# Attention with unnormalised probabilities: values multiplied in PSUM by inverse denominators spread through memory

## What is computed

```python
q = _rope(_rmsnorm(q, q_norm_w), pos); k = _rope(_rmsnorm(k, k_norm_w), pos)
k_all = jnp.concatenate([kc, k], axis=1); v_all = jnp.concatenate([vc, v], axis=1)
scores = jnp.einsum('bqhd,bkhd->bhqk', q, k_all) * SCALE
scores = jnp.where(valid[:, None, None, :], scores, -1e+30)
probs = jax.nn.softmax(scores, axis=-1)
o = jnp.einsum('bhqk,bkhd->bqhd', probs, v_all)
return jnp.einsum('bse,de->bsd', o.reshape(bsz, seqlen, HQ * D), Wo)
```

## Time and profile before

| | before |
|---|---|
| median of 3 runs | 1417.21 us |
| the profiled execution's own time | 1418.94 us |
| its span | 1417.3 us |
| mean granted clock of TensorE | 0.991 |
| TensorE busy | 1363.1 us |
| DVE busy | 1104.8 us |
| ACT busy | 838.1 us |
| GpSimd busy | 456.1 us |

### The profile page before, as it was taken

How to read it: one execution, slowest core, us unless ns; L and a number is a source line. 1 busy time by engine, 2 the same in 40 slices (tenths; PEclk the granted TensorE clock), 3 DMA queues, 4 the chain that set the end, 5 groups by cost and what they waited for, 6 DMA issues and landing times.

```text
span 1417.3 us, 27566 instructions
## 1 busy us (share of the span) xinstructions
PE 1363.1 (96%) x7308; PEld 1157.6 (82%) x7308; DVE 1104.8 (78%) x2921; ACT 838.1 (59%) x1952; POOL 456.1 (32%) x485
## 2 busy tenths in 40 slices
PE   5999999989999999999999999999999999999995
PEld 4888888878888887888888877888888888888884
DVE  4532445869888889888888898888888988888883
ACT  5631334346666667756666677666657676666663
POOL 4000000355222336523333275222224552223320
PEclk9999999999999999999999999999999999999998
DMA  8111213372222235322222443222224522222210
GB/s 307 58 60 46 74 38 124 119 261 54 63 63 63 61 76 159 93 60 59 59 65 69 120 136 68 60 75 62 62 60 132 135 60 59 67 59 59 59 25 14
DMA packets 139828, 118.55 MB, mean 84 GB/s; under 512 B 90240, under 2 KB 109056, under 8 KB 139520
## 3 DMA queue, kind: packets, MB, share of 16 engines
q1 hardware_dynamic: 127328, 83.35, 21.1%
q0 software_dynamic: 11728, 34.09, 9.8%
q10 hardware_dynamic: 720, 0.54, 0.1%
HBM read 101.11 MB, written 16.78 MB: 83 GB/s over the span
## 4 chain that ended last, share of the span: by engine, by line
PE 85%; DVE 6%; issue 6%; ACT 1%; DMA 1%; POOL 0%; SPq 0%; DVEq 0%; POOLq 0%; ACTq 0%
PE bank L1399 16%; PE tail L1438 15%; PE wide L1468 12%; PE tail L1518 12%; PE wide L1433 8%; PE wide L422 4%; PE bank L1420 3%; PE wide L490 3%; PE tail L422 2%; PE bank L422 2%; PE wide L549 2%; DVE pr L1780 1%; PE bank L549 1%; PE bank L490 1%; PE tail L1491 1%
## 5 line engine op out<-in xcount | busy, mean ns | idle before, releaser
L1594 ACT ACTIVATE pr<-pr,nm,q_scale 128x640 f32<-128x640 f32 x256 | 235.6, 921 | 114.7 <-DVE nm L1763 113.8
L1438 PE MATMUL tail<-prT,vt 128*128 128x512 f32 x960 | 254.0, 404 | 4.2 <-DVE prT L1738 4.1
L1759 DVE CUSTOM_DVE_ANT_0 pr<-wide,bias 128x640 f32<-128x640 f32 x256 | 209.8, 819 | 13.6 <-issue 13.6
L1199 POOL TENSOR_TENSOR tick<-tick 128x1 f32<-128x1 f32 x127 | 30.1, 237 | 584.7 <-PE wide L1468 325.1
L1438 PEld LDWEIGHTS tail<-prT,vt 128*128 128x128 f32 x960 | 170.4, 188 | 44.5 <-DVE prT L1738 13.8
L1518 PE MATMUL tail<-woT,oT 128*128 128x512 f32 x768 | 197.2, 400 | 0.0
L1738 DVE TENSOR_TENSOR prT<-wide,prT 128x1024 fp32r<-128x1024 f32 x128 | 153.5, 1220 | 28.6 <-ACT prT L1586 27.8
L1468 PE MATMUL wide<-kT,qT 128*128 128x320 f32 x512 | 163.7, 320 | 4.4 <-DVE mx L1759 4.2
L1518 PEld LDWEIGHTS tail<-woT,oT 128*128 128x128 f32 x768 | 140.5, 189 | 27.1
L1468 PE MATMUL wide<-kT_low,qT 128*128 128x320 f32 x512 | 158.8, 310 | 0.0
L1468 PE MATMUL wide<-kT,oT 128*128 128x320 f32 x512 | 158.6, 310 | 0.0
(11 more groups left out here) (237 smaller groups left out, 2656.9 us busy)
## 6 DMA issues: line engine op xcount, KB each, us to landing
w_ring<-pair_weights SPq DMA_DIRECT2D x80, 256.0 KB, 3.8
k_raw<-k_pages SPq DMA_DIRECT2D x512, 32.0 KB, 2.1
v_raw<-v_pages SPq DMA_DIRECT2D x512, 32.0 KB, 1.7
xTb<-x_transposed POOLq DMA_DIRECT2D x31, 512.0 KB, 4.5
out<-y POOLq DMA_DIRECT2D x32, 256.0 KB, 4.0
rope<-rope_tables SPq DMA_DIRECT2D x31, 256.0 KB, 2.6
w_raw<-w_gate_up SPq DMA_DIRECT2D x10, 512.0 KB, 3.3
x_transposed<-xh SPq DMA_DIRECT2D x8, 512.0 KB, 4.6
```

The lines of the kernel that those rows point to most:

```text
L1438: last = nc.tensor.matmul(tail[g][:, :], vt[v_part][:, j, g * D:(g + 1) * D], prT[p_part][:, j, :], start=(j == 0 and v_part + p_part == 0 ...
L1594: ac.activation(pr[h][:, :], pr[h][:, :], ACT.Exp, bias=nm[:, h:h + 1], scale=q_scale[:, 0, head(h)], accum_out=den[:, h:h + 1]).then_inc( ...
L1759: v.tensor_tensor_reduce(halves(pr[h][:, :]), scores, halves(bias[:, :]), 1.0, -3.0e38, ALU.add, ALU.max, mx[:, h:h + 1]).then_inc(s_sfree, 1)
```

## The change

The probabilities stay as the exponential leaves them. The eight reciprocals are one operation on `den`, at the start of the next turn's back half on DVE. ACT stores them to a scratch tensor in memory (128 rows of eight values) and, after four of the squares, loads the whole of it back into every partition (`spread`, 4 KB each, over the place of the first two probability tiles). When the values of a key head are summed, DVE multiplies them in PSUM by `spread`, whose operand steps over the eight heads, and ACT and DVE then take high and low parts as before, ACT waiting for the multiplication. The low part of the second values stands after the first product of the second rotation. GpSimd waits for fewer things. The casts of weights on ACT are regrouped. In the "next" turn TensorE's ahead projections follow the common table. The pair loop is written out, three times, for PE, DVE and ACT. The semaphores of the probabilities go; three are new.

```diff
+    share_scratch = nc.dram_tensor("one_over_denominators", [P * HP], F32).ap()
...
+    spread = place(135168, "spread", [P, P, HP])
...
-    NSTEP = 22
+    NSTEP = 16
...
-    EARLY = {"next": ((0,), (1, 2, 3), (4, 5, 6, 7), (8,), (9,), (10,)), "out": ((), (), (), (12, 13), (14,), (15,)), None: ((),) * 6}
+    EARLY = {"next": ((0,), (1,), (2, 3), (4, 5, 6, 7), (8,), (9,), (10,)), "out": ((), (), (), (), (12, 13), (14,), (15,)), None: ((),) * 7}
...
-        with eng.Fori(0, NPAIR - 1) as pair:
+        for pair in range(NPAIR - 1):
             with eng.Fori(0, B - 2) as last:
...
             pool.wait_ge(s_sfull, u * HP + HP)
-            pool.wait_ge(s_p[0], u * SOON + FIRST)
...
                 pool.wait_ge(s_step, u * NSTEP + MASKED)
-                low_weights(own, first + 2, first + 3)
+                low_weights(own, first + 2, first + 4)
...
             if extra:
-                for h in range(REP):
-                    pool.wait_ge(s_p[0], u * SOON + h + 1 + FIRST)
-                    low_weights(own, first + 3 + h, first + 4 + h)
-                low_weights(own, first + 3 + REP, first + 2 * KT)
-
-        TURNED, MASKED = 2, NSTEP - SOON
+                low_weights(own, first + 4, first + 2 * KT)
+
+        TURNED, MASKED = 2, NSTEP
...
             def probs_wide(g, w):
 
-                pe.wait_ge(s_p[0], u * SOON + (SOON if g else REP) + FIRST)
-                if g:
-                    pe.wait_ge(s_p[1], u * LATE + LATE + FIRST)
+                pe.wait_ge(s_exp, u * HP + (HP if g else REP))
...
-                        ahead_to = AHEAD_NEXT if extra == "next" else AHEAD
-                        project_ahead(ahead_to[h], ahead_to[h + 1])
+                        project_ahead(AHEAD[h], AHEAD[h + 1])
...
             def copy_values(g):
-                act.wait_ge(s_pv, u * G + g + 1 + FIRST)
+                act.wait_ge(s_norm, u * G + g + 1)
                 ac.copy(oT[:, 0, g, :], tail[g][:, :]).then_inc(s_ohi, 1)
...
             if back:
                 high_probs(0, 0)
+                act.wait_ge(s_rden, u + 1)
+                act.dma_start(share_scratch.rearrange("(p h) -> p h", h=HP), rden[:, :]).then_inc(s_den, 16)
                 high_probs(0, 1)
 
                 act.wait_ge(j_full, u + 1)
                 ac.copy(prT[0][:, JT - 1, :], tail[1][:, :]).then_inc(s_phi, 1)
-                for h in range(SOON, HP):
-                    normalise(u, h)
             if front:
 
                 act.wait_ge(s_q0, n + 1)
                 squares(1, 0, REP)
+            if back:
+                act.wait_ge(s_den, u * 16 + 16)
+                act.dma_start(spread[:, :, :].rearrange("p q h -> p (q h)"),
+                              share_scratch.rearrange("(o n) -> o n", o=1).to_broadcast([P, P * HP])).then_inc(s_spread, 16)
...
             if back:
+                early(0)
                 high_probs(1, 0)
-                early(0)
+                early(1)
                 high_probs(1, 1)
...
+            def shares():
+
+                dve.wait_ge(s_exp, u * HP + HP)
+                v.reciprocal(rden[:, :], den[:, :]).then_inc(s_rden, 1)
+
+            def normalise(g):
+
+                dve.wait_ge(s_pv, u * G + g + 1 + FIRST)
+                if g == 0:
+                    dve.wait_ge(s_spread, u * 16 + 16)
+                summed = tail[g][:, :].rearrange("p (i q) -> p i q", i=REP)
+                v.tensor_tensor(summed, summed, spread[:, :, g * REP:(g + 1) * REP].rearrange("p q i -> p i q"), ALU.mult).then_inc(s_norm, 1)
...
             if back:
+                shares()
                 low_probs(0, 0)
...
                 low_probs(1, 1)
+                normalise(0)
                 low_new(1)
                 low_values(0)
...
             if back:
 
-                low_values(1)
+                normalise(1)
+                if not front:
+                    low_values(1)
             if front:
 
-                rotate(REP + G, REP, ((REP + G, REP, 0),)).then_inc(s_rope, 1)
+                rotate(REP + G, REP, ((REP + G, REP, 0),), (lambda: low_values(1)) if back else None).then_inc(s_rope, 1)
...
-                dve.wait_ge(s_p[1], n * LATE + FIRST)
                 for h in range(HP):
-                    mask_max(h, lambda: reciprocal(h - 2) if h >= 2 else None)
-                    if 2 <= h < REP + 2:
-                        normalise(h - 2)
-                for h in range(REP, SOON):
-                    normalise(h)
-                reciprocal(HP - 2)
-                reciprocal(HP - 1)
+                    mask_max(h)
```

More of the change, by code:

```diff
@@ L273, in build_program @@
                                     tick, xT, xh, x_tok, rope_all, token_place, s_x1, s_xl, s_ropemade, s_ropest, s_xs, s_init, m_full, m_free, s_grp,
-                                    x_scratch, rope_scratch, out)
+                                    x_scratch, rope_scratch, share_scratch, out)
         with nc.Block() as block:
@@ L1024, in build_attention @@
                     tick, xT, xh, x_tok, rope_all, token_place, s_x1, s_xl, s_ropemade, s_ropest, s_xs, s_init, m_full, m_free, s_grp,
-                    x_scratch, rope_scratch, out):
+                    x_scratch, rope_scratch, share_scratch, out):
     def place(offset, name, shape, dt=F32):
@@ L1082, in build_attention @@
     s_rden = sem("denominator_ready")
-    s_p = [sem(f"probs_ready{i}") for i in range(G)]
+    s_den = sem("one_over_denominators_stored")
+    s_spread = sem("one_over_denominators_spread")
+    s_norm = sem("values_normalised")
     s_pv = sem("values_summed")
@@ L1595, in exponential @@
                               accum_out=den[:, h:h + 1]).then_inc(s_exp, 1)
[L1597 to L1602, removed]
             def new_keys_values(n):
@@ L1629, in turn @@
                 squares(1, 0, REP)
+            if back:
+                act.wait_ge(s_den, u * 16 + 16)
+                act.dma_start(spread[:, :, :].rearrange("p q h -> p (q h)"),
+                              share_scratch.rearrange("(o n) -> o n", o=1).to_broadcast([P, P * HP])).then_inc(s_spread, 16)
+            if front:
                 arrive()
@@ L1651, in turn @@
                 copy_values(0)
-            early(1)
+            early(2)
             own = BACK[0] if back else 0
@@ L1655, in turn @@
                 copy_values(1)
-            early(2)
+            early(3)
             if front:
                 high(1, 2, qT[:, 0, :], bank[1][:, :])
-                early(3)
+                early(4)
                 high(0, 3 + own, kT[:, :, L:NK], bank[0][:, 0:G * S].rearrange("p (g c) -> p g c", g=G))
-                early(4)
+                early(5)
                 high(1, 3, qT[:, 1, :], bank[1][:, :])
-                early(5)
+                early(6)
             if back:
@@ L1729, in rotate @@
                     v.tensor_tensor(o, q, cos_w.to_broadcast([P, m, D]), ALU.mult)
+                    if between:
+                        between()
                     v.tensor_tensor(s[:, :, 0:half], q[:, :, half:D], sin_w[:, :, 0:half].to_broadcast([P, m, half]), ALU.mult)
@@ L1767, in mask_keys @@
                 then(v.tensor_scalar(bias[:, 0:L], key_no[:, :], seq_f[:, bass.ds(b, 1)], NEG, ALU.is_ge, ALU.mult))
-            def reciprocal(h):
-                dve.wait_ge(s_exp, n * HP + h + 1)
-                last = v.reciprocal(rden[:, h:h + 1], den[:, h:h + 1])
-                if h < SOON:
-                    at.inc(last)
-                else:
-                    last.then_inc(s_rden, 1)
-            def normalise(h):
-                dve.wait_ge(s_step, n * NSTEP + (NSTEP - SOON + h + 1))
-                v.tensor_scalar(pr[h][:, :], pr[h][:, :], rden[:, h:h + 1], None, ALU.mult).then_inc(s_p[0], 1)
+            def shares():
[7 more added lines that the diff above has]
+                v.tensor_tensor(summed, summed, spread[:, :, g * REP:(g + 1) * REP].rearrange("p q i -> p i q"), ALU.mult).then_inc(s_norm, 1)
             def low_values(g):
```

10 lines of the change are left out of this document (3 added, 7 removed).

## The result

The changed kernel takes 1467.87 us, the median of four runs (1464.51 to 1472.36). The kernel before took 1417.80 beside it (four runs, 1412.75 to 1420.72). The ratio is 1.0359 (95% interval 1.0318 to 1.0401): 50 us or 3.6% slower. The span of the profiled execution is 1467.2 against 1417.3, and the mean granted clock 0.989 against 0.991.

The account below looks back on a forecast made before the run. TensorE, busy 96% of the span, was taken as the bound. Ordinary turns +43.2, "next" -1.5, "out" +0.8, jump -4.3, first turn -1.5, last -2.4 sum to +34.3 us: median 1451.5, near 1452, range 1430 to 1478.

Parts of the forecast that it names:

- TensorE has no gap in an ordinary turn, so removed work gives nothing there: 25 of 31 turns: TensorE busy all 33.50 us, so removing DVE or ACT work gains nothing.
- Part 2, the duration of the multiplication: Values normalised in PSUM: two 0.95 us multiplies delay TensorE's second half of the output projection, 1.73 us per ordinary turn.
- The bound from below: Multiply as short as a same-size one with contiguous operands, 0.68 us: gap 1.19 us, total 1435.
- "Next" turns, -0.5 each: Three turns before a new pair: 1.73 us new gap less 2.24 recovered, about -0.5 us each.
- The recovery of 2.24 in the score stretch: Score stretch of "next" turns: without the stretched DVE multiplication the masked maxima keep up, and 2.24 us go.
- Part 3, store and load at no cost: Denominators through memory: load lands near 713.1, DVE asks at 714.97, nearly 2 us to spare, cost nothing.
- Rival (a): Load lands late and DVE stands at the first multiply, 0.9 us late: +28 us, 1480; chance 0.13.
- "Out" turns, +0.28 each: Three turns after a new pair: 1.73 us new gap less their whole 1.45 surplus, +0.8 us in all.
- Part 5, the jump, -4.3: Pair loop written out: the turn behind its jump loses 2.16 us, twice, 4.3 us saved.
- First turn -1.5, last -2.4: Removed multiplications lay on the chain, up to 2.17 us in the first turn, 2.70 in the last; savings 1.5 and 2.4.

Follow-up runs that it names:

- an edit that the forecast didn't think of: Changed kernel with the multiplication walked queries outside, heads inside, so SBUF is read in runs of four words and PSUM stepped by 128 words: 1436.16 us, ratio 1.0149.

## Why the prediction was right, and where its sizes were off

The forecast was 1452 in a range of 1430 to 1478, with the multiplications' chain as its cause; measured is 1467.87. Mechanism, place and releaser hold for the ordinary turns, which make most of the time. By its own steps:

- **TensorE has no gap in an ordinary turn, so removed work gives nothing there.** Right: without multiplications, but with everything removed that the change removes, the ordinary turn is 33.5 as before.
- **Part 2, the duration of the multiplication.** This is the mis-sized term. The forecast took 0.95, the middle of 0.68 and 1.22; measured are 1.20 and 1.12, near the upper end. Its own sum with these two, 1.73 + 0.25 + 0.17, gives a gap of 2.15, measured 2.03. With 0.69 it gives 1.21, measured 1.13. So the chain was right to about 0.1 us, and the ordinary turns account for 7.5 of the 15.6 us that were missed (49.9 - 34.3): 25 x (2.03 - 1.73). The Trainium skill's rule ("Vector Engine (DVE) Microarchitecture Reference", "Measured stream behaviour on trn2") pointed in the right direction: by its figure, which is for a hop of 4 KiB, one hopping source would cost an estimated 0.35 us here. The runs show 0.465 for a step of eight words. The bound from below was met by an edit that the forecast didn't think of, and at it the forecast's sum (1435) stands beside a measured 1436. That closeness is partly luck: the "next" turns of that run are 2.5 us longer in all than before, where the sum had them 3.2 shorter, the terms around the first turn came out lower than forecast, and the kernel before took 1414.77 in that job.
- **"Next" turns, -0.5 each.** The step that failed: they got 1.4, 2.5 and 3.0 longer. The recovery of 2.24 in the score stretch was worth having (34.8 without multiplication, against 38), but the new gap there was costed as in an ordinary turn, the load as free, and the clock at nothing. Before, one gap of 1.83 us stood in front of the keys' transposes. Now two of 1.52 and 1.68 stand in a row, with two stretched root steps between the multiplications, and the granted clock fell in all three turns where it had fallen in one. Of the 8.4 us missed here the clock is about 4.3 (the estimate above), the load's waits are 2.0, the longer multiplications 3 x 0.30. The rest, about 1.2, isn't traced. Taking store and load away leaves most of it. What makes the clock fall isn't shown: it fell in no "next" turn without multiplications and in two of the three with the step in PSUM, but in none of the run with VectorE reordered, which has gaps as long, and with the loop kept it stayed up in one turn with the same two gaps.
- **Part 3, store and load at no cost.** Right in 28 of 31 turns, wrong by 0.1 us in one and by 1.0 in two, worth about 2 us in all by the turns of the run without them. Rival (a) had the place right only for "next" turns, in which w_ring's loads are under way beside it. Its price doesn't come out of its own terms: 705.2 + 5.2 for the store and 4.5 with the issue for the load is 715.2 to 715.5, 0.2 to 0.5 us late and not 0.9.
- **"Out" turns, +0.28 each.** Measured +0.6, which is the ordinary turn's own extra 0.30: they did come down to the common length.
- **Part 5, the jump, -4.3.** Right: -4.2 by itself on the kernel before. In the changed kernel it is worth only about 2.6 by the turns (1.3 each), and the totals don't show it at all. Probably DVE's idle of 3.2 is partly covered by slack that the kernel before hadn't.
- **First turn -1.5, last -2.4.** Measured -2.8 and -2.3. The forecast capped the first by a still low clock, but in the trace before, the clock is at 0.50 only up to 314.5 us, ahead of the 2.17 on the chain at 319.26. The term was taken too low, but with the same code ahead of it the start of that turn's back half lies between 321.9 and 327.6 us among the variants, so the term can't be told from the scatter.

Together: 7.5 us from the ordinary turns, 8.4 from the "next" turns, 1.0 from the "out" turns, and about 1.2 back from the first, the last and the jump.

## What to carry to other kernels

Before moving elementwise work from a place with slack to a smaller one without, count what the chain there already holds: here two operations and two hand-offs on a chain with 1.05 us of slack cost more than the eight removed operations gave. Try the walk of an operand that puts the step into the other memory, and fill only measured idle time: small steps moved ahead helped where the engine stood waiting and harmed where they delayed a second consumer. Where some turns have another engine at work beside the chain, cost it there with the stretched durations, and look at the granted clock turn by turn before comparing such turns.

## What the runs showed of the hardware

- A DVE multiplication of 128x512, input and output in PSUM, with the SBUF input stepped by eight 4-byte words takes 1.07 to 1.20 us; in one run, or in runs of four words with both PSUM streams stepped by 128 words, 0.69.
- Tiny DVE operations (128x10) take 1.2 us in place of 0.17 while GpSimd splits weights, two or three in a row, in the "next" turns of every run.
- A broadcast load of 512 KB from ACT's queue lands in 4.5 us (median), and in up to 8.6 in the turns in which loads of 256 KB run beside it.
- The granted clock fell to 0.50 around TensorE idles of 1.52 and 1.68 us close together in all three "next" turns of the changed kernel. In the kernel before it stayed at 1.00 behind one idle of 1.83 and fell behind one of 1.78. With the loop kept it stayed at 1.00 behind 1.58 and 1.61 once. The length of the idle alone doesn't decide it.
- The loop's jump left DVE idle for 2.64 to 3.20 us; written out, the turns behind a pair change had the ordinary length (33.46 and 33.50).
